# Strassen sums of U3 and C22 half by half, layer norm of the next pair earlier, refinement later among the fragments: a GNN kernel on one core

## What is computed

```python
h = maximum(layernorm(x), 0)
x = x + L0(h)      # h <- relu(adj*adj @ h @ W1); relu(. @ W2); . @ W3, each with adj*adj
h = maximum(layernorm(x), 0)
x = x + L1(h)      # agg = U.T @ h; out = relu(agg @ V1 + b1) @ V2 + b2; U @ out
```

## Time and profile before

| | |
|---|---|
| median of three runs | 2367.04 us (2366.0 to 2368.21) |
| the profiled execution | 2365.93 us, span 2364.1 us |
| busy: TensorE matmuls | 2297.2 us (97%) |
| busy: VectorE | 2011.3 us (85%) |
| busy: ScalarE, GpSimd | 1104.8 and 1103.9 us (47% each) |
| one matmul instruction of 256 columns, mean | 379 to 384 ns by group |
| mean granted clock of TensorE | 0.999 |
| chain that ended last | TensorE 72%, VectorE 15%, ScalarE 4%, GpSimd 3% |

### The profile page before, as it was taken

One profiled execution on the slowest core, in us unless ns is written; L12 is line 12 of the kernel. 1 busy time (PEld: TensorE's weight loads), 2 busy tenths in 40 slices (PEclk: granted clock), 3 DMA queues, 4 the chain that ended last, 5 costly groups with the idle time before them and its releaser, 6 DMA issues.

```text
span 2364.1 us, 44376 instructions
## 1 busy us (share of the span) xinstructions
PE 2297.2 (97%) x11052; PEld 1881.5 (80%) x11052; DVE 2011.3 (85%) x10270; ACT 1104.8 (47%) x2582; POOL 1103.9 (47%) x1780
## 2 busy tenths in 40 slices
PE   5999999999999999999999999999999998999999
PEld 3778777777788777777877778887788887889998
DVE  6999999999999888777788889799999997447776
ACT  3454554545555444544444444444444443244554
POOL 4445454444455555555444465445555444243332
PEclk9999999999999999999999999999999999999999
DMA  2000000000000000000000000000000001014443
GB/s 101 28 28 10 27 19 27 27 28 27 28 27 14 24 27 27 28 18 27 27 28 27 27 27 27 27 10 27 27 27 27 27 27 36 18 50 138 132 133 108
DMA packets 90009, 89.82 MB, mean 38 GB/s; under 512 B 5376, under 2 KB 89088, under 8 KB 89856
## 3 DMA queue, kind: packets, MB, share of 16 engines
q1 hardware_dynamic: 89856, 88.23, 11.7%
HBM read 54.66 MB, written 33.55 MB: 37 GB/s over the span
## 4 chain that ended last, share of the span: by engine, by line
PE 72%; DVE 15%; ACT 4%; issue 4%; POOL 3%; SPq 0%; DMA 0%; POOLq 0%; ACTq 0%; DVEq 0%
PE ps L1462 57%; PE ps L1640 10%; PE ps L1376 2%; DVE A L878 2%; POOL hid2T L522 2%; DVE A L882 2%; DVE xrow_sb L887 1%; ACT squares L616 1%; PE ps L1650 1%; ACT root_s L618 1%; DVE prods L915 1%; ACT hid2T L676 1%; PE ps L1587 1%; DVE sc L896 1%; DVE ps L930 1%
## 5 line engine op out<-in xcount | busy, mean ns | idle before, releaser
L1462 PE MATMUL ps<-w,hid2T 128*128 128x256 f32 x2048 | 473.6, 381 | 20.8 <-ACT hid2T L676 20.5
L1462 PEld LDWEIGHTS ps<-w,hid2T 128*128 128x128 f32 x2048 | 375.0, 190 | 86.4 <-ACT hid2T L676 33.2
L464 POOL COPY Eb<-sc 128x1 f32 (+1 forms) x254 | 47.3, 186 | 528.5 <-DVE v L903 292.8
L1462 PE MATMUL ps<-agg2T,w 128*128 128x256 f32 x1024 | 242.2, 379 | 0.0
L1462 PE MATMUL ps<-hid2T,xin 128*128 128x256 f32 x1024 | 239.0, 380 | 1.6 <-POOL adjT L500 1.6
L1462 PE MATMUL ps<-weightT,hid 128*128 128x256 f32 x1024 | 234.2, 379 | 0.0
L1462 PE MATMUL ps<-w,aggT 128*128 128x512 f32 x512 | 231.2, 592 | 0.0
L1075 DVE RECIPROCAL ps<-ahead 128x40 f32<-128x40 f32 (+1 forms) x768 | 217.9, 329 | 0.1
L1462 PEld LDWEIGHTS ps<-weightT,hid 128*128 128x128 f32 x1024 | 190.1, 191 | 33.1 <-issue 10.7
L1462 PEld LDWEIGHTS ps<-hid2T,xin 128*128 128x128 f32 x1024 | 190.1, 190 | 27.6 <-ACT h2T L669 1.9
L1462 PEld LDWEIGHTS ps<-agg2T,w 128*128 128x128 f32 x1024 | 188.5, 190 | 25.1
(11 more groups left out here) (369 smaller groups left out, 5494.1 us busy)
## 6 DMA issues: line engine op xcount, KB each, us to landing
xl<-in_x_dram SPq DMA_DIRECT2D x64, 256.0 KB, 2.9
xr<-in_x_dram SPq DMA_DIRECT2D x64, 256.0 KB, 2.9
x_dram<-xr SPq DMA_DIRECT2D x64, 256.0 KB, 2.3
xin<-x_dram SPq DMA_DIRECT2D x64, 256.0 KB, 2.8
out_dram<-xin SPq DMA_DIRECT2D x64, 256.0 KB, 2.2
w<-in_L_gnn_W_dram SPq DMA_DIRECT2D x1, 2048.0 KB, 10.1
w<-in_L_gnn_W_dram SPq DMA_DIRECT2D x1, 1024.0 KB, 11.4
w<-in_L_gnn_W_dram SPq DMA_DIRECT2D x1, 512.0 KB, 3.7
```

The lines of the kernel that those rows point to most:

```text
L464: pool.tensor_copy(Eb[:, bass.ds(k, 1)], sc[:, 4:5])
L1462: ins = pe.matmul(dst, a, b, start=start, stop=stop)
```

## The change

The additions U3 and C22 are interleaved by half. The second image's layer norm begins in step 3 of a pair instead of step 5; in the pairs without steps both images' layer norm parts are moved ahead. The refinement's seven products start six fragments later (18 becomes 24, and so on), the second transposes at fragment 56 instead of 54 and the eigenvectors at 60 instead of 58. No operation is added or removed. `placed` and `ADD_AT` follow the new `ADDS`: in eleven-step pairs C22's first half stands ahead of U3's second in step 6; in twelve- and fourteen-step pairs C22's first half moves up beside U3's first, and one addition moves up a step.

```diff
--- before.py
+++ after.py
@@ -205,7 +205,7 @@
         sums_ready, turn_s, added, fin = sem("sums_ready"), sem("turn_s"), sem("added"), sem("fin")
         s_out, fin_ready, shifted, stored = sem("s_out"), sem("fin_ready"), sem("shifted"), sem("stored")
 
-        LN_AT = (1, 5)
+        LN_AT = (1, 3)
         FROM_ONE = (v_saved, house_v, sturm_v, vec_v, evac, x1_ready, fin_ready)
         primer = sb("primer", [P, len(FROM_ONE)])
 
@@ -231,7 +231,7 @@
         PAIRS = B // 2
 
 
-        REFINE_AT, TURN_AT, VECTORS_AT = (18, 20, 23, 27, 29, 32, 36), 54, 58
+        REFINE_AT, TURN_AT, VECTORS_AT = (24, 26, 29, 33, 35, 38, 42), 56, 60
         FIRST_ROUND = WITH_STEPS + 2
 
 
@@ -306,7 +306,9 @@
 
 
         S_TURNS = [(n, half) for half in range(2) for n in (1, 2, 3, 4)]
-        ADDS = [(name, half) for name in ("U2", "C11", "U4", "U3", "C22", "C12", "C21") for half in range(2)]
+        ADDS = [(name, half) for name in ("U2", "C11", "U4") for half in range(2)]
+        ADDS += [(name, half) for half in range(2) for name in ("U3", "C22")]
+        ADDS += [(name, half) for name in ("C12", "C21") for half in range(2)]
         LAST_OF = {"U2": "P6", "C11": "P2", "U4": "P5", "U3": "P7", "C22": "P7", "C12": "P3", "C21": "P4"}
         FINS = [(name, half) for name in ("C11", "C22", "C12", "C21") for half in range(2)]
         ADD_AT = {a: n for n, a in enumerate(ADDS)}
@@ -572,10 +574,11 @@
                 for n in range(1, 5):
                     sum_of_moving(pair, n)
                 for n in range(len(ADDS)):
-                    if more and n % 4 == 0 and n < 8:
-                        ln_minus_mean(pair + 1, n // 4)
-                    if more and n % 4 == 2 and n < 8:
-                        ln_scale(pair + 1, n // 4)
+                    if more and n == 0:
+                        for j in range(2):
+                            ln_minus_mean(pair + 1, j)
+                    if more and n in (2, 4):
+                        ln_scale(pair + 1, n // 2 - 1)
                     add_products(pair, n)
 
             with pool.Fori(WITH_STEPS, PAIRS - 1) as t:
@@ -749,7 +752,7 @@
                                              bias=rs[:, j, 3, r:r + 1], scale=rs[:, j, 1, r:r + 1])
                     ins.then_inc(h2_ready, 1)
 
-            LN_AFTER = {0: [(0, 0)], 3: [(1, 0)], 4: [(0, 1)], 5: [(2, 0)], 7: [(1, 1)], 9: [(2, 1)]}
+            LN_AFTER = {0: [(0, 0)], 1: [(0, 1)], 3: [(1, 0)], 4: [(1, 1)], 6: [(2, 0)], 7: [(2, 1)]}
             FINS_AFTER = {9: [0, 1], 11: [2], 12: [3], 13: [4, 5, 6, 7]}
 
             def pair_body(pair, more, joins=False, norms=False):
```

## The result

The changed kernel takes 2377.73 us (median of five, 2377.09 to 2378.5) against 2366.68 (2366.0 to 2368.21) for the kernel before on the same chip: a ratio of 1.0044, 95% interval 1.0034 to 1.0055. It is slower by 11 us; 2367.8 was forecast, with 2360 to 2373.5 as the range.

The account below looks back on a forecast made before the run. TensorE, busy 2297 of 2364 us, bounds the kernel; only its holes can be won. Terms -8.92 + 11.95 + 3.7 + 2.2 - 3.5 - 3.1 - 1.6 = +0.7 us on median 2367.04: 2367.8, range 2360 to 2373.5.

Parts of the forecast that it names:

- edit 3: LN_AT (1, 5) to (1, 3), pairs 0 to 20: +3.7, +2.2, -3.5 and -3.1 us; pairs 0 to 3 nothing.
- the bounds of pairs 4 to 10: Nothing if ScalarE has run ahead; 0.75 us more per pair if GpSimd loses half its own layer norm block.
- edit 4: U3 and C22 half by half, and the pure pairs' layer norm: order gives nothing, filled GpSimd idle time -1.6 us.
- the sign chain: VectorE work before the second transposes: 19.4 us unhindered, 34.0 with 15 GpSimd additions costing 0.97 each.
- P6's wait: TensorE's P6 waits for GpSimd's second moving sum: +3.7 us in pairs 4 to 10, +2.2 in pairs 11 to 17.
- Edit 1: Refinement's seven entries six fragments later: the wait before Z's first transposes and its slow clock go, -8.92 us.
- Edit 2: Second transposes at 56, eigenvectors at 60: TensorE waits 10.1 us, with clock loss 1.85, together +11.95 us.
- Rival 1: Wait before the second transposes stays short: 5.1 us instead of 11.95, total 2360.9; chance 0.25.
- rival 2: VectorE makes no progress under a GpSimd addition: 4.4 us more, total 2372.2; chance 0.08.
- rival 4: Wait before the first transposes not removed, Z over 3.3 us later: by 2 us more, total 2369.8; chance 0.05.
- g3's wait: TensorE's third product waits for C12's second half in pairs 11 to 17: 0.50 us each goes, -3.5 us.
- rival 3: P6 waits longer, second moving sum 0.75 us later in each of 14 pairs: +10.5, total 2378.3; chance 0.07.

Follow-up runs that it names:

- the kernel with all of it: Changed kernel with qn reading zero from PSUM, GpSimd's moving sums first, refinement products at 22 to 40, second transposes 61, eigenvectors 65: 2343.47 us, ratio 0.9902.

## Why the prediction was wrong, point by point

**The step that failed.** It is edit 3's "In pairs 0 to 3 an apply replaces squares of equal length: 0", and with it the bounds of pairs 4 to 10, which speak of P6 and GpSimd's own block alone, and edit 4's "So the order gives nothing". All three asked who waits for GpSimd's moved work; none asked what GpSimd now does in the moments that the edits shift or free, and on what VectorE operation that falls. The mechanism was in the prediction, and the earlier trace rows, with its price, 0.97 us a meeting, and was applied to the sign chain only. qn is such an operation, two elements from SBUF to SBUF, and the kernel before shows it held, at 0.77 in step 6 of pairs 4 to 10. What it measured: qn is 6.7 us longer in pairs 0 to 3, which grew by 7.1 with the slow clock in pair 1, and pairs 4 to 10 grew by 7.4 us with P6's wait, in place of 0 and 3.7. With these two terms the forecast's sum is 2367.8 + 6.7 + 3.7 = 2378.2; that this is within 0.5 of the measured time is partly luck, since the later stages are off by up to 1.6 us each, some up and some down, and these errors offset each other. That qn is the cause is shown by the kernel in which it alone is freed.

The Trainium skill, SBUF — State Buffer, section "Who interferes with whom", says that a `tensor_scalar` can run in a two-port mode, that VectorE in such a mode and GpSimd then exclude each other, the one that issues first holding the shared ports for its whole instruction, and that an operation with at most one SBUF input outside these modes does not contend. The Trainium skill's page VectorE: DVE Perf Modes, section "Mode 2×_2P — use both read ports for one tensor", wants one source, it and the destination in SBUF, and an outermost non-unit dimension that is even, or odd and equal in both. The runs agree: held with two columns in SBUF (0.22 becomes 1.26), free with a PSUM operand, held with two SBUF inputs. That section does not say what holds for one column, where no non-unit dimension is left; the run shows it free. The prediction named the first page and drew from it only a rival for the sign chain.

**Edit 1** was right: -8.92 forecast. In the kernel with all of it, where both waits are gone, the stretch from pair 30 to the end takes 394.7 us against 403.7: 8.9 less.

**Edit 2** was right in kind and too large by 1.6. In the changed kernel the end takes 405.1, 10.4 more than without waits; forecast was 11.95. The chain took 32.1 us from the last correction's end, not 34.3, though 15 additions and moving sums did fall into it, as forecast:

```profile
2056.89 0.69 DVE L1239 TENSOR_TENSOR Zt<-Zt,ps 128x512 f32<-128x512 f32 x1 [7.40 <-PE ps L1590]
2061.02 1.27 POOL L511 TENSOR_TENSOR hid2T<-agg2T,hid2T 128x512 f32<-128x512 f32 x1 [5.63 <-ACT agg2T L672]
2061.08 1.23 DVE L1262 TENSOR_SCALAR sgn<-sgn 128x2 f32<-128x2 f32 x1
2062.35 0.69 DVE L1253 TENSOR_REDUCE lev<-Zsq 128x16 f32<-128x512 f32 x1
2081.88 2.48 POOL L524 TENSOR_TENSOR hid2T<-h2T,hid2T 128x512 f32<-128x512 f32 x2
2088.82 1.11 PE L1602 MATMUL ps<-ident,Z 128*128 128x128 f32 x4 [7.79 <-DVE Z L1281]
```

Some of them met reductions, as the one that began at 2062.25 did, and cost nothing; in the mean, with the prediction's 19.4 us for the chain unhindered and 31.9 for it here, each cost (31.9 - 19.4) / 15 = 0.83 us, not 0.97. The clock fell as forecast: the five microseconds up to 2090, in which TensorE mostly stood, have a granted clock of 0.55 (the third column from the end), a mixture of 1.2 and 2.4 GHz.

```profile
2085.00:2090.00 5.00, 1.18 (x5) 1.19 (x6) 4.48 (x21) 0.00 (x0) 0.00 (x0) 0.55 0.00 0
```

The four transposes and the 32 instructions behind them took from 2088.82 to 2098.16, 9.3 us; in the kernel with all of it as many take 7.3. The loss is 2.0, forecast 1.85. Rival 1 (a short second wait) and rival 2 (no progress at all) both fell, and rival 4 too: the first transposes came without a wait.

**Edit 3** in pairs 11 to 20 came out in its numbers: P6's price 2.3 (forecast 2.2) in pairs 11 to 17, net -2.0 (-1.3); -3.4 (-3.1, where three times 1.0 is 3.0) in pairs 18 to 20. But these gains are not LN_AT's alone. By itself it gives 1.9 and 1.8 us there, and the order, which the prediction put at nothing, gives 2.1 and 0.9: either edit removes g3's wait in pairs 11 to 17, and the halving of the second wait in pairs 18 to 20 is the order's. P6 in pairs 4 to 10 was 2.3 rather than 3.7: its waits show 0.50 us in pair 4 and 0.25 in pair 9, some 3.8 in all with the hidden 0.16, and 1.5 of that, not 0.8, replaced other waits (the prediction's 4.5 was also more than the 4.0 that a line from 0.75 to 0.4 over seven pairs gives); rival 3, P6 waiting longer, fell, though the time that it gave, 2378.3, came true by another mechanism.

**Edit 4**: the order costs 1.2 us in pairs 21 to 29 by itself, the layer norm parts give 1.1; together -0.3, forecast -1.6.

The four parts run alone or read out, 2.2 (places), 8.75 (LN_AT), 2.5 (order) and -1.4 (layer norm in the free pairs, without the part that the first wait's end takes away), give 12.1; the change measured 11.05. The small difference hides two larger ones: in pairs 4 to 10 LN_AT and the order cost 5.4 and 5.7 alone and 7.4 together, and in pairs 11 to 17 they give 1.9 and 2.1 alone, by the same wait, and only 2.0 together.

## What to carry to other kernels

When work is moved on GpSimd, go through what each engine beside it is doing at the moments that are filled, not only through who waits for the moved result. Two cases are to be looked for: GpSimd waits for a signal from VectorE, so that its next operation begins together with VectorE's next ones (step 7 here); or GpSimd is late and still at the work of the step before (steps 4, 6 and 8). In both the same small operation can be met in every round, so list VectorE's small operations with two elements or more, source and destination in SBUF, around that signal. A cheap cure is to let such an operation read one operand from PSUM; and a gain found in one place of a kernel with such meetings can be lost in another, so judge an edit stage by stage.

## What the hardware showed beyond expectation

- A `tensor_scalar` of 128x2 from SBUF to SBUF took 0.22 us alone and up to 1.28 beside a 128x512 GpSimd addition of 1.27; the same with 128x1 took 0.21 at most in 74 meetings.
- One operation of two elements per partition, made to read a zero from PSUM instead of SBUF, is worth 7.0 us of 2367 in the kernel before and 19.6 in the changed one.
- One more operation of 0.2 us in each of 128 two-block steps cost 9.6 us.
- After waits of 0.77 and 2.01 us in one pair, with 2.4 us of matmuls between them, the granted clock was 0.57 over the next 4 us and twelve instructions took 4.54 us instead of 2.86; after waits of 0.77 and 1.97 at the same place a pair later it stayed at 1.00.
